# A fused cross-attention and expert-FFN kernel: row normalisation of the first stage on GpSimd in place of DVE

## What is computed

```python
def _layernorm(x, axis=-1, eps=1e-05):
    m = jnp.mean(x, axis=axis, keepdims=True)
    v = jnp.var(x, axis=axis, keepdims=True)
    return (x - m) / jnp.sqrt(v + eps)
...
q = _split_heads(Q @ Wq.T + bq, B, S)       # Q = _layernorm(x), K = V = ctx
k = _split_heads(K @ Wk.T + bk, B, S)
v = _split_heads(V @ Wv.T + bv, B, S)
scores = jnp.einsum('bhqd,bhkd->bhqk', q, k) * scale
probs = jax.nn.softmax(scores, axis=-1)
out = jnp.einsum('bhqk,bhkd->bhqd', probs, v)
...
x = x + (out @ Wo.T + bo)
...
logits = xf @ Wr.T + br                     # xf = _layernorm(x)
expert_idx = jnp.argmax(logits, axis=-1)
h = jax.nn.relu(jnp.einsum('td,efd->etf', xf, W1) + b1[:, None, :])
y = jnp.einsum('etf,edf->etd', h, W2) + b2[:, None, :]
x = x + y[expert_idx, jnp.arange(xf.shape[0])]
```

## Time and profile before

| | |
|---|---|
| median of 3 runs | 562.91 us (560.3 to 563.98) |
| the profiled execution | 563.26 us, span 561.3 us |
| PE busy | 472.0 us, 84% |
| DVE busy | 408.6 us, 73% |
| ACT busy | 310.0 us, 55% |
| POOL busy | 235.0 us, 42% |
| mean granted TensorE clock | 0.939 |

### The profile page before, as it was taken

One profiled execution on the slowest core, in us unless ns is written; L12 is line 12 of the kernel. 1 busy time (PEld: TensorE's weight loads), 2 busy tenths in 40 slices (PEclk: granted clock), 3 DMA queues, 4 the chain that ended last, 5 costly groups with the idle time before them and its releaser, 6 DMA issues.

```text
span 561.3 us, 19186 instructions
## 1 busy us (share of the span) xinstructions
PE 472.0 (84%) x6467; PEld 356.3 (63%) x6468; DVE 408.6 (73%) x1053; ACT 310.0 (55%) x584; POOL 235.0 (42%) x391
## 2 busy tenths in 40 slices
PE   1999968899989899898998989760099999999992
PEld 1666634566656566565665656650099999999991
DVE  6789555687978789787987878543457777778771
ACT  1677745565655555555565654300067777777770
POOL 6233212212226437255273562735524444454442
PEclk9999979999999999999999998955579999999997
DMA  7355100000011101111021110920212222222220
GB/s 248 114 151 149 40 19 18 17 18 18 17 20 45 27 22 49 21 35 36 14 58 22 33 30 1 356 76 24 87 50 68 65 69 65 65 65 66 66 60 0
DMA packets 32480, 33.74 MB, mean 60 GB/s; under 512 B 6419, under 2 KB 25750, under 8 KB 32160
## 3 DMA queue, kind: packets, MB, share of 16 engines
q1 hardware_dynamic: 28096, 24.33, 16.3%
q0 software_dynamic: 4320, 8.53, 4.5%
HBM read 19.10 MB, written 9.99 MB: 52 GB/s over the span
## 4 chain that ended last, share of the span: by engine, by line
PE 56%; DVE 15%; issue 13%; POOL 7%; ACT 5%; DMA 2%; SPq 1%; DVEq 0%; POOLq 0%
PE PS L918 12%; PE PS L931 11%; PE PS L796 7%; PE PS L809 5%; DVE SB L635 4%; DVE MX L627 4%; ACT SB L494 4%; PE PS L780 3%; PE PS L879 3%; PE PS L785 3%; POOL rows L425 3%; PE PS L767 3%; PE PS L888 3%; PE PS L904 1%; PE PS L844 1%
## 5 line engine op out<-in xcount | busy, mean ns | idle before, releaser
L403 POOL TENSOR_TENSOR VP<-BIG,C 128x128 f32<-128x128 f32 x128 | 56.1, 460 | 155.7 <-PE PS L888 152.8
L796 PEld LDWEIGHTS PS<-C,SB 128*128 128x128 f32 x512 | 55.2, 143 | 80.8 <-ACT SB L494 66.9
L627 DVE TENSOR_REDUCE MX<-PS 128x16 f32<-128x1024 f32 x64 | 78.2, 1222 | 38.3 <-PE PS L809 37.2
L435 POOL DMA_INDIRECT out<-SB,BIG x71 | 69.0, 972 | 82.3 <-DVE SB L751 79.2
L796 PE MATMUL PS<-C,SB 128*128 128x128 f32 x512 | 85.4, 290 | 18.4 <-ACT SB L494 12.7
L510 ACT COPY KM<-BIG 128x644 f32 x71 | 51.8, 729 | 55.0 <-PE PS L918 29.2
L494 ACT ACTIVATE SB<-SB 128x1024 f32<-128x1024 f32 x64 | 67.7, 1058 | 23.5 <-DVE SB L635 23.0
L918 PE MATMUL PS<-BIG,KM 128*128 128x128 f32 x568 | 79.8, 282 | 0.4
L635 DVE TENSOR_TENSOR SB<-PS,MX 128x1024 f32<-128x1024 f32 x64 | 77.4, 1209 | 1.7
L931 PE MATMUL PS<-KM,SB 128*128 x568 | 76.0, 277 | 0.6 <-ACT SB L514 0.6
L918 PEld LDWEIGHTS PS<-BIG,KM 128*128 128x128 f32 x568 | 71.8, 195 | 3.0 <-issue 1.7
(11 more groups left out here) (108 smaller groups left out, 690.8 us busy)
## 6 DMA issues: line engine op xcount, KB each, us to landing
BIG<-rows SPq DMA_DIRECT2D x71, 66.0 KB
X<-in_x SPq DMA_DIRECT2D x16, 256.0 KB, 3.2
PT<-in_ctxT SPq DMA_DIRECT2D x16, 256.0 KB, 2.8
KM<-BIG SPq DMA_DIRECT2D x256, 16.0 KB
BIG<-in_we SPq DMA_DIRECT2D x1, 2576.0 KB, 12.7
KM<-in_w SPq DMA_DIRECT2D x1, 2048.0 KB, 9.0
out<-SB,BIG POOLq DMA_INDIRECT x71
rows<-X,DESTI POOLq DMA_INDIRECT x64, 2.4
```

The source lines that it names most:

```text
L403: last = nc.gpsimd.tensor_tensor(dst, v, own, ALU.mult)
L435: nc.gpsimd.indirect_dma_start(out=out, out_offset=bass.IndirectOffsetOnAxis(ap=RT[:, s.r, ID:ID + 1].bitcast(i32), axis=0), in_=YO[:, s.r ...
L627: nc.vector.tensor_reduce(MX[:, n % 2, :], sc, axis=AX.X, op=ALU.max).then_inc(mx_done, 1)
L796: last = nc.tensor.transpose(bank(4)[:, i * P:(i + 1) * P], SB[:, n % 2, hp * P:(hp + 1) * P], ident)
```

## The change

GpSimd normalises the rows of stage 1. Its program for the stage is written out for all groups where it was a loop, and in step n it normalises group n and then adds the bias to group n-1. DVE keeps the statistics, the moments and the reciprocal. RSTD gets two slots, and DVE waits for a slot's last reader (`xn_done` at n-1) before it takes the reciprocal. The wait for the transposes that free an XN slot (`xt_done`) goes from DVE to GpSimd.

```diff
-        SD, RSTD = sb("SD", P, 2, GT), sb("RSTD", P, GT)
+        SD, RSTD = sb("SD", P, 2, GT), sb("RSTD", P, 2, GT)
...
-            pool.wait_ge(bo_ready, 1)
-            def add_bias(s):
-                pool.wait_ge(xn_done, s.n + 1)
-                g = X[:, bass.ds(s.n * GT, GT), 0:D]
-                nc.gpsimd.tensor_tensor(g, g, BO.unsqueeze(1).to_broadcast([P, GT, D]), ALU.add).then_inc(xb_done, 1)
-            steps(pool, 0, NG, 2, add_bias)
+            def normalise(n):
+                if n < NG:
+                    pool.wait_ge(rstd_done, n + 1)
+                    need(pool, xt_done, n - 1)
+                    for t in range(GT):
+                        last = nc.gpsimd.tensor_scalar(XN[:, n % 2, t, :], X[:, n * GT + t, 0:D], MV[:, n % 2, 0, t:t + 1],
+                                                       RSTD[:, n % 2, t:t + 1], ALU.subtract, ALU.mult)
+                    last.then_inc(xn_done, 1)
+                if n >= 1:
+                    if n == 1:
+                        pool.wait_ge(bo_ready, 1)
+                    pool.wait_ge(xn_done, n)
+                    g = X[:, (n - 1) * GT:n * GT, 0:D]
+                    nc.gpsimd.tensor_tensor(g, g, BO.unsqueeze(1).to_broadcast([P, GT, D]), ALU.add).then_inc(xb_done, 1)
+            for n in range(NG + 1):
+                normalise(n)
...
-                need(dve, done, n)
+                need(dve, *done)
                 dve.wait_ge(sd, n + 1)
                 nc.vector.reciprocal(inv, root).then_inc(rstd, 1)
-                dve.wait_ge(rstd, n + 1)
...
-                    need(dve, xt_done, b.n - 1)
-                    xb = X[:, bass.ds(b.n * GT, GT), 0:D]
-                    inverse(b.n, RSTD[:], SD[:, b.r % 2, :], sd_done, rstd_done, xn_done)
-                    for t in range(GT):
-                        last = normalise(XN[:, b.r % 2, t, :], xb[:, t, :], MV[:, b.r % 2, 0, t:t + 1], RSTD[:, t:t + 1])
-                    last.then_inc(xn_done, 1)
+                    inverse(b.n, RSTD[:, b.r % 2, :], SD[:, b.r % 2, :], sd_done, rstd_done, (xn_done, b.n - 1))
```

More of the change, by code:

```diff
@@ L535, in inverse @@
             def inverse(n, inv, root, sd, rstd, done):
-                need(dve, done, n)
+                need(dve, *done)
                 dve.wait_ge(sd, n + 1)
                 nc.vector.reciprocal(inv, root).then_inc(rstd, 1)
-                dve.wait_ge(rstd, n + 1)
-            def normalise(dst, src, mean, inv):
-                return nc.vector.tensor_scalar(dst, src, mean, inv, ALU.subtract, ALU.mult)
             def stage1(s):
```

## The result

The changed kernel takes 581.67 us (median of 4 runs, 580.37 to 582.26) against 561.62 us for the kernel before in the same comparison (also the median of 4): a ratio of 1.0349, 95% interval 1.0303 to 1.0395. It is slower by about 20 us, outside the range of the prediction. The profiled execution took 582.0 us, its span is 580.0 us, 18.7 more than before.

What follows compares the result with a forecast made beforehand. PE was taken to bound stage 1 at 3.43 us a group; -1.0 us at the start and +0.3 in the loop gave -0.7, forecast 562.2 us from a median of 562.91, range 560 to 572.

Steps and rivals of the forecast that it cites:

- What GpSimd pays: Stage 1 on GpSimd: 64 tensor_scalar, 415 ns each taken; load 2.55 us of 3.43 a group.
- pitch p: Time from one GpSimd normalising instruction to the next: 0.365 us taken, bounds 0.24 and 0.41.
- rival 2: Stage 1's loop through GpSimd and DVE sets the pace from p = 0.34; +9.7 us at p = 0.55; chance 0.25.
- rival 3: GpSimd's normalising instruction slow altogether: p = 1.04, period 6.24 us, +38 us, 601 us; chance 0.06.
- The added chain: Stage 1 loop: normalisations, bias, DVE's moments and reciprocal, signal; period 4p + 2.08, 3.54 us against PE's 3.43; +0.3 us.
- the lead: Slack before PE's transposes that stage 1's loop uses up first: 2.62 - 4p, 1.16 us at p = 0.365.
- The load: GpSimd's busy time per stage 1 group: 2.55 us of 3.43, fitting up to p = 0.58.
- The start: Before 12.27 us: L570 right behind L539, so PE's L761 and K projection begin earlier; gain 1.0 us, at least 0.5.
- the cover: Group 0's transposes come at about 13.6 us; GpSimd's four normalisations, 11.0 to some 12.5, stay ahead up to 0.6 us apiece.
- Moved for nothing: End of stage 1: the later bias and moved waits cost nothing; 1.5 us of cover before GpSimd's L403 at 70.09.
- rival 4: Granted clock dip between 71 and 80 us moves or is spared: 2 us either way; chance 0.04, half a gain.
- the estimate that spoke against the change: GpSimd's normalising instruction by the skill: 290 ns plus 170 for two column operands, 460 ns; sum +1.5 us.

Runs made afterwards that it cites:

- forms run: Changed kernel with other forms of the normalising instruction in pairs of groups 4 to 13 (fewer columns, constants, halves, copy); executed once, 574.73 us, read for its instructions only.
- four-slot run: Changed kernel with four slots for MV and RSTD in place of two, so DVE's moments wait less for normalisations; 572.62 us, ratio 1.0208 to the kernel before.
- run of the start alone: Kernel before, with DVE completing the output bias right behind group 0's reciprocal, ahead of its normalisations, nothing on GpSimd; 559.87 us, ratio 0.9970.
- kernel with both edits: Changed kernel with two tensor_tensor per group for the normalisation and four slots for MV and RSTD; 560.45 us, ratio 0.9985 to the kernel before.

## Why the prediction was wrong

**The step that failed** is the size of one term of the sum, in "What GpSimd pays": "I take the 415 ns ... and so a pitch p of 0.365 us (bounds 0.24 and 0.41)". The instruction takes 792 ns and its pitch is 3.12/4 = 0.78. I took a bound "from above, at equal size" from a two-input tensor_tensor (L403), as if a tensor_scalar with two columns couldn't cost more. Nothing in the rows gave that: they hold a cast, memsets and tensor_tensor on GpSimd, and the forms run shows tensor_scalar in a class of its own, 235 ns over a copy with one constant and one operation. The far end that I named, 1.04, held it, but I worked rival 2 out to p = 0.55 only and gave rival 3, p = 1.04, a chance of 0.06; the range ended at 572 us, which is p = 0.54. Why a tensor_scalar costs 235 ns more than a copy on this engine stays open.

**The added chain** was right, and it is rival 2 that came, in its place and with its workings. The period of 4p + 2.08 gives 5.20 at p = 0.78; measured 5.04. The parts: the four normalisations 3.12 (3.17 by the form), the bias with L535's end 1.08 (1.04 predicted), from the end of L535 to the reciprocal's end 0.72 and in every fourth group 0.83 (0.84 predicted), the signal 0.10 (0.15). The four-slot run shows that the loop hung on the two slots of MV, the run without the bias that the bias stood in it: GpSimd's load was then below PE's 3.43 us, and the period still 4.2. It fell by 0.83 us and not by the whole 1.05 of the bias, since the first moments instruction, which had run under the bias, then adds its own part.

**The size.** By rival 2's own form with p = 0.78 the lead, 2.62 - 4p, is -0.5, and one gets 13 x (5.20 - 3.43) + 0.5 - 1.0 = +22.5 us; measured +20. With the measured period, 12 groups x 1.61 = 19.3, and 0.73 for the last group, whose reciprocal had long been taken (period 4.16), make 20.0. The stage as a whole was 21.8 longer; the other 1.7 us lie ahead of group 2's transposes, for which the prediction's sum had nothing: 0.76 to group 0's transposes (with their wait for POOL), 0.61 to group 1's (L785 took 1.89 us where it took 1.34 before, so the slow early pace lasted longer), 0.33 to group 2's. Against them stand the 1.74 by which L761 came earlier.

**The load** alone, "it fits, up to p = 0.58", would have been broken as well: 4.17 us of busy time a group against PE's 3.43. With four slots it is what is left.

**The start** was right: 1.0 us predicted. In the changed kernel L570 began 0.09 us after the reciprocal did, before 1.23 (10.70 and 11.93); the other 0.58 of the 1.74 by which L761 came earlier is that the second group's x landed sooner (statistics at 8.52 against 9.10); no run shows the change to have a part in that. So PE's start is as predicted. What follows it is not: the cover that I named for the transposes of group 0, "up to 0.6 us apiece", was overrun by the longer normalisations: they waited 0.56 us for POOL, and with the 1.7 us above the gain was gone by group 2 (22.89, against 22.93 before). The run of the start alone has the gain without that.

**Moved for nothing** held. The last two biases ended at 89.63, L413 began at 90.17 as V's copy landed, and DVE's stage 2 with L627 at 92.38. The dip of the clock stayed, 0.81 of full, so rival 4 had no part in what stage 1 lost; the 1.65 us that the last stage was shorter are of its kind, and the run of the start alone shows that the dip behind stage 1 can be missing.

**By the Trainium skill.** The page GPSIMD Engine Reference of the Trainium skill (section 4.1) has one-input work at roughly line-rate. The copy, 292 ns, doesn't speak against that, but tensor_scalar does: 527 ns in its simplest form, and 3.4 ns an element in its full one. Its 102 cycles for a small read (section 7), by an estimate 85 ns at the 1.2 GHz that the page gives the engine, lie near what the columns cost, 74 ns each; that the columns are such reads is not shown. So the estimate that spoke against the change had its own term nearly right and lacked the larger ones, as my sum did. (By the prediction's own form its 460 ns give +1.8 us, as under rival 2, and not the +1.5 written beside it.)

## What to carry to other kernels

An instruction form that an engine doesn't run in the trace has no upper bound in its neighbours: give it a range up to several times the nearest row, or measure that one form first, before anything is built on it. When a producer's last step moves to another engine, look for the buffer slots that order closed for free; a double buffer that was never waited on becomes a loop through both engines, and its length is the sum of both engines' parts with whatever else stands in either stream, not the larger load. And take the part of such a change that needs no engine at all: here the only gain that a run shows, about 1.5 us, was one instruction's place in DVE's stream.

## What the runs showed of the hardware

- On GpSimd, 128x128 f32 (all from the forms run): copy 292 ns, tensor_scalar with one constant 527, two constants 645, one column 602, two columns 793; two tensor_tensor of 128x512 with broadcast operands do the work of four tensor_scalar in 2.16 us in place of 3.12 (the run with two long instructions).
- DVE's moments instructions begun beside a GpSimd tensor_tensor last until it ends (L535 846 ns on the mean in the changed kernel; L539 1.01 us and L542, a tensor_scalar with one SBUF input, 1.02 us in the kernel with both edits). Beside a GpSimd tensor_scalar they were hardly held: in the four-slot kernel two-input L536 and L537 ran in 0.17 and 0.16 us, and GpSimd's instructions kept their length (median 787 ns). By the Trainium skill (SBUF — State Buffer, on the shared port pair) any GpSimd instruction that reads SBUF should have held the two-input ones; here the measurement decides, and it says so only of this form.
- In the kernel before, the two-input L525 of group 0 took 0.17 us (at 4.39) beside the memset of the first microseconds, where L530, a tensor_scalar on DVE, took 3.82 us, up to 8.56; the memsets ended at 8.54.
- The dip of the granted clock behind stage 1 is not in every execution: 0.78 in the 9 us from 71 in the profiled execution before, 1.00 in that of the start alone.
